# The first two query tiles made together, half of y at a time

## The chip, the cores and the metric

The kernel runs on one core of one Trainium2 chip. The metric is the device time of one execution in microseconds (us), lower is better. One execution was taken by the hardware profiler; its page, its trace and its own time are what the text below reads.

## The reference, cut to what matters

32 sequences of 32 tokens with 512 features go through one block of attention and a small feed-forward part, all in fp32. What the change touches is the step from x to the queries:

```
y   = x @ W.T + b + 2 * (x @ A[slot]) @ B[slot]     # base and adapter, slot per sequence
q   = rope(y @ Wq)      # 32 heads of 16
k,v = rope(y @ Wk), y @ Wv                          # 8 groups
ctx = softmax(mask(q k^T) / 4) v
x1  = x + ctx @ Wo
out = x1 + gated low-rank experts of x1             # top 2 of 4, through a second adapted product
```

## The kernel before

The work is cut into 4 groups (g) of 8 sequences, 256 tokens each. Features lie on the 128 partitions, so y of a group is 4 blocks (c) of 128 features by 256 tokens, and so is q: 4 tiles. To keep fp32 accuracy with the fast matmul type, each operand of a large product is held as a high part and a low part (what the high part leaves), and each product is three matmuls: high x high, high x low, low x high.

One y block therefore goes this way. TensorE sums it in PSUM (`y_base`, L1014, then `y_adapter`, L1022); blocks 0 and 1 are the halves of bank FR[0], blocks 2 and 3 those of FR[1]. ScalarE writes the high part with the bias (`y_high`, L338, matmul type, semaphore yT_h), VectorE the low part (`y_low`, L648, semaphore yT_l, one increment per block). `q_tile` (L1038) then multiplies with Wq over all four blocks: tiles 0 and 1 go to the halves of FR[0], which the y low parts of blocks 0 and 1 have just freed, tiles 2 and 3 to FR[1]. It waits until the low parts of all four blocks are there. The second tile of each bank raises q_ps. ScalarE then swaps partitions into qx (`q_swap`, L351, four copies), VectorE multiplies with cosine and sine, GpSimd adds (`q_sum`), and `scores` begins when all of q is there. `kv_tile` (L1048) makes k and v from the same y.

Each engine works through a list of steps in a fixed order that is written out by hand, one list per engine, with the groups interleaved: while group g is in its attention part, y of group g+1 is summed. An engine that waits holds back all that is listed behind. Around the change TensorE's list is:

- group 0: `y_adapter(0, 0)`, `y_adapter(0, 1)`, `keep_clock(6, ZB)` (six matmuls on zeros, in the profile the tile `still`), then the four q tiles, the two kv tiles and `y_base(1, 0)`
- group 1: `y_adapter(1, 1)`, `scores(0, 1)`, `p_transposes(0, 0, ZB)`, then the four q tiles
- group 2: two kv tiles, `scores(1, 1)`, `mid_logits` and `p_transposes` of earlier groups, then the q tiles
- group 3: `kv_tile(3, 1)`, then the q tiles

Other steps that the text names: ScalarE's list in group 1 is y_high(1, 0), y_high(1, 1), exp(0, 1), x_high(2, 0), wo_high(3), pt_copy(0, 0), x_high(2, 1), q_swap(1, 0), exp(0, 2), q_swap(1, 1), exp(0, 3), pt_copy(0, 1), kv_copy(1), k_swap(1). VectorE's `mask` and `top` mask the scores and take their maximum, GpSimd's `shift` (L530) subtracts it, ScalarE's `exp` (L374) follows, VectorE's `sums` (L714), GpSimd's `norm` (L525), and `p_transposes` (L1102) on TensorE. `x_low` (L639) is VectorE's low part of the next group's x. `mid_logits` (L1162) needs rows that SyncE loads for each label (`load_labels`, L196).

Of the kernel before, what the change touches and what calls it, by code (L numbers as in the profile page):

```python
# [15 lines left out]
KT = D // P  # L16
G = 4
SEQ = B // G
TOK = SEQ * T
# [43 lines left out]
def program(nc, xt, xn, idt, wt, wq, wkv, wo, w2, mix_in, small_in, lA, lB, consts, out):  # L63
    ctx = ExitStack()
    with ctx:
        def sb(name, shape, dt=F32):
            return ctx.enter_context(nc.sbuf_tensor(name, shape, dt))

        def sem(name):
# [9 lines left out]
        Wq = [sb(f"Wq{i}", [P, KT, PH, P], F32R) for i in "hl"]  # L79
# [13 lines left out]
        yS = [sb(f"yT{i}", [P, KT, TOK], F32R) for i in "hl"]  # L93
# [44 lines left out]
        FR, SMALL, SC, YB, ZB, XB = bank[0:2], bank[2], bank[3:5], bank[5], bank[6], bank[7]  # L138
# [11 lines left out]
        WT_h, WT_l, Wq_h, Wq_l, Wkv_h, Wkv_l, Wo_h, Wo_l, BT_l, xT_h, xT_l, yT_h, yT_l, cT_l = map(  # L150
            sem, "WT_h WT_l Wq_h Wq_l Wkv_h Wkv_l Wo_h Wo_l BT_l xT_h xT_l yT_h yT_l cT_l".split())
        h_ps, h_sb, y_half, y_ps, q_ps, q_sb, kv_ps, kv_sb, kx_sb, k_sin, q_sin, k_cos, q_cos = map(
            sem, "h_ps h_sb y_half y_ps q_ps q_sb kv_ps kv_sb kx_sb k_sin q_sin k_cos q_cos".split())
# [809 lines left out]
        def _(pe):  # L963
# [3 lines left out]
            def mm3(dst, lhsT, rhs, start, stop):  # L967
                mm(dst, lhsT[0], rhs[0], start, False)
                mm(dst, lhsT[0], rhs[1], False, False)
                return mm(dst, lhsT[1], rhs[0], False, stop)  # L970

            def keep_clock(n, dst):
                pe.wait_ge(blank, 1)
                for _ in range(n):
                    mm(dst[:, 0:P], still[:], still[:], True, True)
# [62 lines left out]
            def q_tile(g, q):  # L1038
                if g == 0:
                    pe.wait_ge(Wq_l, KT)  # L1040
                pe.wait_ge(yT_l, KT * (g + 1))
                dst = FR[q // 2][:, (q % 2) * TOK:(q % 2 + 1) * TOK]
                for c in range(KT):
                    i = mm3(dst, [w[:, c, q] for w in Wq], [z[:, c] for z in yS], c == 0, c == KT - 1)
                if q % 2:
                    i.then_inc(q_ps, 1)

            def kv_tile(g, n):  # L1048
                if g == 0:
                    pe.wait_ge(Wkv_l, 2)  # L1050
                pe.wait_ge(yT_l, KT * (g + 1))
                for c in range(KT):
                    i = mm3(SMALL[:, TOK * n:TOK * (n + 1)], [w[:, c, n] for w in Wkv], [z[:, c] for z in yS], c == 0, c == KT - 1)
                if n:
                    i.then_inc(kv_ps, 1)
# [46 lines left out]
            def p_transposes(g, j, dst):  # L1102
                if g == 0 and j < 2:
                    pe.wait_ge(RL_sb, KT)
                if 0 < g < G - 1 and j >= 2:
                    pe.wait_ge(fin_sb, TT * g)
                pe.wait_ge(normed, PAIRS * g + j + 1)
                for s in range(4):
                    i = tr(dst[:, P * s:P * (s + 1)], flat(ex[:, j])[:, P * s:P * (s + 1)])
                i.then_inc(pt_ps, 1)  # L1110
# [105 lines left out]
            y_adapter(0, 0)  # L1216
            y_adapter(0, 1)
            keep_clock(6, ZB)
            q_tile(0, 0)
            q_tile(0, 1)  # L1220
            q_tile(0, 2)
            q_tile(0, 3)
            kv_tile(0, 0)
            kv_tile(0, 1)
            y_base(1, 0)
            fold_router(0)
# [15 lines left out]
            y_adapter(1, 1)  # L1242
            scores(0, 1)
            p_transposes(0, 0, ZB)
            q_tile(1, 0)
            q_tile(1, 1)
            q_tile(1, 2)
            q_tile(1, 3)
            kv_tile(1, 0)
            p_transposes(0, 1, YB)  # L1250
            kv_tile(1, 1)
# [21 lines left out]
            mid_logits(0, 1, XB)  # L1273
            p_transposes(1, 0, ZB)
            p_transposes(1, 1, YB)
            q_tile(2, 0)
            q_tile(2, 1)
            q_tile(2, 2)
            q_tile(2, 3)
            v_spread(2)  # L1280
# [23 lines left out]
            mid_logits(1, 1, XB)  # L1304
            p_transposes(2, 0, ZB)
            kv_tile(3, 1)
            q_tile(3, 0)
            q_tile(3, 1)
            q_tile(3, 2)
            p_transposes(2, 1, YB)  # L1310
            mid_transpose(1, 0, XB)
# [90 lines left out]
```

## Time and profile before

| | |
|---|---|
| median of 3 runs | 161.06 us (160.15 to 162.93) |
| profiled execution, its own time | 160.41 us |
| its span, first to last instruction | 158.4 us |
| busy: TensorE, VectorE, ScalarE, GpSimd | 146.2, 99.4, 76.3, 65.3 us |
| mean granted TensorE clock | 1.000 |

Times in rows are microseconds from the start of the span, unless a row says ns. PE is TensorE, PEld its weight loads, DVE VectorE, ACT ScalarE, POOL GpSimd, SP SyncE (SPq: its issuing of DMAs). L with a number is a line of the kernel; where a helper issues an instruction the line is the helper's (L965 for most matmuls, L310 for copies on ScalarE). A timeline row is start, duration, engine, line, operation, output<-inputs, shapes and count; consecutive instructions alike are merged, and a bracket at the end is the idle time before them and what ended it. x4 means four instructions in a row. A fp32 matmul that is not of the fast type counts as two.

### The profile page before, as it was taken

The numbers are of one execution on the slowest core, as the hardware profiler recorded it, in microseconds if no ns is written. First come the engines' busy times: TensorE is split into PE (matmuls) and PEld (weight loads), VectorE is DVE, ScalarE is ACT, GpSimd is POOL, SyncE is SP. The second block draws the span as 40 slices with busy tenths as digits, with TensorE's granted clock in tenths as the row PEclk, the third lists the DMA queues.
The fourth block names the chain that finished last, engine by engine and source line by source line (L and its number), as shares of the span: only waits on it lengthen the run. The fifth ranks groups of instructions, "written<-read, shape, count | busy, mean of one in ns | idle before, by whom it ended". The sixth has DMA issues, their size and how long they took to land.

```text
span 158.4 us, 5011 instructions
## 1 busy us (share of the span) xinstructions
PE 146.2 (92%) x1970; PEld 135.1 (85%) x1970; DVE 99.4 (63%) x227; ACT 76.3 (48%) x152; POOL 65.3 (41%) x70
## 2 busy tenths in 40 slices
PE   6986699999979999999999999999999899789991
PEld 6985699998969998999999898999997689568761
DVE  0584455428849873166689794867838588708692
ACT  4642479921155994205397904261696450621410
POOL 1700000196252459620965584362774567610000
PEclk9999999999999999999999999999999999999999
DMA  5999993112154112430210013320002532134015
GB/s 143 370 289 387 411 388 70 37 41 45 41 169 153 43 42 58 135 115 0 84 57 0 4 55 117 107 73 4 0 0 76 201 110 106 39 114 136 1 66 199
DMA packets 14536, 17.76 MB, mean 112 GB/s; under 512 B 5762, under 2 KB 10370, under 8 KB 14258
## 3 DMA queue, kind: packets, MB, share of 16 engines
q1 hardware_dynamic: 13282, 15.23, 28.6%
q10 hardware_dynamic: 1040, 2.03, 4.2%
q8 instruction: 15, 0.25, 0.7%
q0 software_dynamic: 192, 0.20, 0.4%
q14 instruction: 7, 0.06, 0.1%
HBM read 10.90 MB, written 2.10 MB: 82 GB/s over the span
## 4 chain that ended last, share of the span: by engine, by line
PE 73%; DVE 8%; SPq 4%; ACT 4%; issue 3%; DMA 3%; POOL 1%; POOLq 1%; DVEq 0%
PE bank L965 55%; PE bank L997 12%; PE bank L978 4%; PE bank L1030 3%; DMA B<-lb 3%; DVE yTl L651 2%; DVE x L799 2%; ACT qx L310 1%; SPq L174 1%; SPq L175 1%; DVE mgT L794 1%; ACT yTh L343 1%; POOL qr L558 1%; SPq L177 1%; ACT PT L310 1%
## 5 line engine op out<-in xcount | busy, mean ns | idle before, releaser
L532 POOL TENSOR_TENSOR sm<-sm,mx 128x512 f32<-128x512 f32 x16 | 17.2, 1073 | 27.7 <-DVE mx L712 27.6
L527 POOL TENSOR_TENSOR ex<-ex,ri 128x512 f32<-128x512 f32 x16 | 17.3, 1089 | 10.0 <-DVE ri L718 9.9
L310 ACT COPY qx<-bank 32x512 f32<-32x512 f32 x32 | 18.5, 578 | 4.8 <-PE bank L965 4.3
L965 PE MATMUL bank<-yTh,Wqh 128*128 128x256 f32 x64 | 18.2, 285 | 2.4 <-DVE yTl L651 2.4
L376 ACT ACTIVATE ex<-sm 128x512 f32<-128x512 f32 x16 | 10.1, 633 | 17.1 <-POOL sm L532 16.9
L965 PE MATMUL bank<-yTl,Wqh 128*128 128x256 f32 x64 | 17.9, 280 | 0.0
L965 PE MATMUL bank<-yTh,Wql 128*128 128x256 f32 x64 | 17.9, 279 | 0.0
L997 PE MATMUL bank<-xTh,WTh 128*128 128x256 f32 x64 | 16.4, 289 | 0.0
L997 PE MATMUL bank<-xTl,WTh 128*128 128x256 f32 x64 | 16.1, 282 | 0.0
L310 ACT COPY PT<-bank 128x512 f32<-128x512 f32 (+1 forms) x17 | 9.6, 576 | 13.5 <-PE bank L978 11.8
L997 PE MATMUL bank<-xTh,WTl 128*128 128x256 f32 x64 | 15.9, 279 | 0.0
L707 DVE TENSOR_TENSOR sm<-bank,mixed 128x512 f32<-128x512 f32 x16 | 10.7, 674 | 7.0 <-PE bank L965 5.7
L965 PEld LDWEIGHTS bank<-yTh,Wqh 128*128 128x128 f32 x64 | 12.0, 188 | 2.8 <-issue 1.4
L965 PE MATMUL bank<-cTh,Woh 128*128 128x256 f32 x48 | 13.8, 288 | 0.0
L965 PE MATMUL bank<-cTh,Wol 128*128 128x256 f32 x48 | 13.3, 277 | 0.0
L965 PE MATMUL bank<-cTl,Woh 128*128 128x256 f32 x48 | 13.3, 277 | 0.0
L558 POOL TENSOR_TENSOR qr<-qkc,qks 128x512 f32<-128x512 f32 x8 | 10.5, 1317 | 5.5 <-DVE qkc L725 3.1
L716 DVE TENSOR_REDUCE su<-ex 128x16 f32<-128x512 f32 x16 | 10.8, 677 | 2.2 <-ACT ex L376 2.0
L539 POOL TENSOR_TENSOR qkc<-kv,mixed 128x256 f32<-128x256 f32 x4 | 2.9, 730 | 22.3 <-ACT kv L310 22.3
L965 PEld LDWEIGHTS bank<-yTl,Wqh 128*128 128x128 f32 x64 | 12.0, 188 | 0.0
L965 PEld LDWEIGHTS bank<-yTh,Wql 128*128 128x128 f32 x64 | 12.0, 187 | 0.0
L343 ACT ACTIVATE yTh<-bank,mixed 128x256 fp32r<-128x256 f32 x16 | 6.4, 474 | 11.5 <-PE bank L1030 11.4
(116 smaller groups left out, 396.7 us busy)
## 6 DMA issues: line engine op xcount, KB each, us to landing
RS<-RL SPq DMA_DIRECT2D x32, 136.0 KB, 2.0
xF<-xt SPq DMA_DIRECT2D x8, 256.0 KB, 3.2
out<-x SPq DMA_DIRECT2D x7, 256.0 KB, 2.1
Wqn<-wq ACTq DMA_DIRECT2D x2, 512.0 KB, 5.0
Wqn<-wo SPq DMA_DIRECT2D x1, 1024.0 KB, 6.4
Wn<-w SPq DMA_DIRECT2D x1, 1024.0 KB, 9.0
x<-small SPq DMA_DIRECT2D x1, 904.0 KB, 5.9
A<-la SPq DMA_DIRECT2D x28, 32.0 KB, 1.8
```

Source lines behind the costliest of these rows:

```text
L310: return nc.scalar.copy(dst, src)
L343: nc.scalar.activation(yS[0][:, c, :], FR[h][:, (c % 2) * TOK:(c % 2 + 1) * TOK], ACT.Identity, bias=bias[:, c:c + 1]).then_inc(yT_h, 1)
L376: nc.scalar.activation(flat(ex[:, j]), flat(sm[:, j % 2]), ACT.Exp, scale=HD ** -0.5).then_inc(exped, 1)
L527: nc.gpsimd.tensor_tensor(ex[:, j], ex[:, j], ri[:, j, :, None].broadcast_to((P, 2 * NG, T)), ALU.mult).then_inc(normed, 1)
L532: nc.gpsimd.tensor_tensor(sm[:, j % 2], sm[:, j % 2], mx[:, j, :, None].broadcast_to((P, 2 * NG, T)), ALU.subtract).then_inc(shifted, 1)
L558: nc.gpsimd.tensor_tensor(qr[:, :, s, :].rearrange("p s h t -> p h s t"), qkc[:, s].rearrange("p h (s t) -> p h s t", t=T), qks[:, s].rear ...
L707: V.tensor_tensor(sm[:, j % 2], SC[j % 2][:].rearrange("p (a s) -> p a s", s=T), small(C_CAUSAL, T)[:, None].broadcast_to((P, 2 * NG, T)), ...
L716: V.tensor_reduce(su[:, j], ex[:, j], AX.X, ALU.add).then_inc(summed, 1)
L965: return nc.tensor.matmul(dst, lhsT, rhs, start=start, stop=stop)
L978: return nc.tensor.transpose(dst, src, ident[0:n, 0:n])
L997: nc.tensor.matmul(FR[c // 2][:, (c % 2) * TOK:(c % 2 + 1) * TOK], WT[u][:, k, P * c:P * (c + 1)], xT[r][:, k], start=first, stop=False, s ...
L1030: i = nc.tensor.matmul(FR[b][:, n * TOK + P * e:n * TOK + P * (e + 1)], B1[g % 2][rows, P * (2 * b + n):P * (2 * b + n + 1)], hT[rows, P * ...
```

## The change

In each group q tiles 0 and 1 are made by one function. It goes over the first two blocks of y for both tiles, then over the last two for both. Ahead of each half it waits for the low parts of that half's blocks only. The 24 matmuls are those of the two tiles before, in another order; `start` is set on the first one of the bank alone, and q_ps is raised once at the end, as before. The calls are replaced in all four groups; nothing else changes.

```diff
+            def q_pair(g):
+                if g == 0:
+                    pe.wait_ge(Wq_l, KT)
+                for half in range(2):
+                    pe.wait_ge(yT_l, KT * g + 2 * (half + 1))
+                    for q in range(2):
+                        for c in (2 * half, 2 * half + 1):
+                            for u, r in ((0, 0), (0, 1), (1, 0)):
+                                i = nc.tensor.matmul(FR[0][:, q * TOK:(q + 1) * TOK], Wq[u][:, c, q], yS[r][:, c],
+                                                     start=c == 0 and q == 0 and u == 0 and r == 0, stop=c == KT - 1 and u == 1,
+                                                     skip_group_check=True)
+                i.then_inc(q_ps, 1)
+
...
             keep_clock(6, ZB)
-            q_tile(0, 0)
-            q_tile(0, 1)
+            q_pair(0)
             q_tile(0, 2)
             q_tile(0, 3)
...
             p_transposes(0, 0, ZB)
-            q_tile(1, 0)
-            q_tile(1, 1)
+            q_pair(1)
             q_tile(1, 2)
...
-            q_tile(2, 0)
-            q_tile(2, 1)
+            q_pair(2)
...
-            q_tile(3, 0)
-            q_tile(3, 1)
+            q_pair(3)
```

## Rows read from the trace of the kernel before

**Rows 1.** The page: busy time by engine, and TensorE's granted clock in 40 slices.
```profile
PE 146.2 (92%) x1970; PEld 135.1 (85%) x1970; DVE 99.4 (63%) x227; ACT 76.3 (48%) x152; POOL 65.3 (41%) x70
...
PEclk9999999999999999999999999999999999999999
```

**Rows 2.** The page: chain that ended last, by line.
```profile
PE bank L965 55%; PE bank L997 12%; PE bank L978 4%; PE bank L1030 3%; DMA B<-lb 3%; DVE yTl L651 2%; DVE x L799 2%; ACT qx L310 1%; SPq L174 1%; SPq L175 1%; DVE mgT L794 1%; ACT yTh L343 1%; POOL qr L558 1%; SPq L177 1%; ACT PT L310 1%
```

**Rows 3.** Waits of TensorE: engine, tile and line, releaser, total us, times, longest.
```profile
PE bank L965 <- DVE yTl L651: 2.4, 2, 1.2
```

**Rows 4.** Timeline of TensorE, groups 0 and 1: start, us, what.
```profile
16.43 1.60 PE L965 MATMUL bank<-still 128*128 128x128 f32 x12
19.27 0.36 PE L965 MATMUL bank<-yTh,Wqh 128*128 128x256 f32 x1 [1.24 <-DVE yTl L651]
...
46.09 0.66 PE L978 MATMUL bank<-K,ex 128*128 128x128 f32 x4
47.88 0.38 PE L965 MATMUL bank<-yTh,Wqh 128*128 128x256 f32 x1 [1.13 <-DVE yTl L651]
```

**Rows 5.** Timelines of VectorE and TensorE, group 2.
```profile
73.59 0.88 DVE L651 SCALAR_TENSOR_TENSOR yTl<-bank,mixed,yTh 128x256 fp32r<-128x256 f32 x2 [0.37 <-ACT yTh L343]
...
81.50 0.36 PE L965 MATMUL bank<-yTh,Wqh 128*128 128x256 f32 x1
```

**Rows 6.** Timeline of VectorE, y low parts of groups 0 and 1.
```profile
17.46 0.88 DVE L651 SCALAR_TENSOR_TENSOR yTl<-bank,mixed,yTh 128x256 fp32r<-128x256 f32 x2 [1.76 <-ACT yTh L343]
...
18.65 0.47 DVE L651 SCALAR_TENSOR_TENSOR yTl<-bank,mixed,yTh 128x256 fp32r<-128x256 f32 x1
...
46.16 0.87 DVE L651 SCALAR_TENSOR_TENSOR yTl<-bank,mixed,yTh 128x256 fp32r<-128x256 f32 x2 [1.96 <-ACT yTh L343]
...
47.35 0.47 DVE L651 SCALAR_TENSOR_TENSOR yTl<-bank,mixed,yTh 128x256 fp32r<-128x256 f32 x1
```

**Rows 7.** Timeline of TensorE, products of a q tile.
```profile
19.46 0.28 PE L965 MATMUL bank<-yTl,Wqh 128*128 128x256 f32 x1
...
20.76 0.28 PE L965 MATMUL bank<-yTh,Wqh 128*128 128x256 f32 x1
```

**Rows 8.** Timeline of ScalarE, group 0.
```profile
22.37 2.34 ACT L310 COPY qx<-bank 32x512 f32<-32x512 f32 x4 [1.12 <-PE bank L965]
```

**Rows 9.** Timeline of ScalarE, group 1.
```profile
51.01 2.35 ACT L310 COPY qx<-bank 32x512 f32<-32x512 f32 x4 [1.59 <-PE bank L965]
53.38 0.63 ACT L376 ACTIVATE ex<-sm 128x512 f32<-128x512 f32 x1
54.03 2.35 ACT L310 COPY qx<-bank 32x512 f32<-32x512 f32 x4
```

**Rows 10.** Timelines of GpSimd and VectorE, group 1; durations of L641 (ns, min/median/max).
```profile
48.78 1.05 POOL L527 TENSOR_TENSOR ex<-ex,ri 128x512 f32<-128x512 f32 x1 [2.45 <-DVE ri L718]
52.26 1.05 POOL L532 TENSOR_TENSOR sm<-sm,mx 128x512 f32<-128x512 f32 x1 [2.43 <-DVE mx L712]
...
49.17 1.22 DVE L641 TENSOR_TENSOR xTl<-xF,xTh 128x512 fp32r<-128x512 f32 x1
...
L641 DVE TENSOR_TENSOR xTl<-xF,xTh x8: 679/684/1220, 6.4 to 88.8; 128x512 fp32r<-128x512 f32 x8
```

**Rows 11.** The normalization of the fourth pair, and its transposes.
```profile
59.49 1.05 POOL L527 TENSOR_TENSOR ex<-ex,ri 128x512 f32<-128x512 f32 x1
...
61.21 0.60 PE L978 MATMUL bank<-K,ex 128*128 128x128 f32 x4
```

**Rows 12.** Later steps of group 1 on TensorE and GpSimd.
```profile
65.16 1.04 POOL L564 TENSOR_TENSOR Kbd<-kr,mixed 128x512 f32<-128x512 f32 x1
...
67.57 1.05 PE L965 MATMUL bank<-Kbd,qr 64*128 64x128 f32 x14
```

**Rows 13.** Timelines of TensorE and SyncE, the tail.
```profile
134.65 1.16 PE L965 MATMUL bank<-RS,x 128*32 128x68 f32 x64
...
123.93 13.09 SPq L204 DMA_DIRECT2D RS<-RL  x9
```


## The prediction

> **What bounds the kernel now.** I read the page first. TensorE is busy 92% of the span, the next engine 63%, and the granted clock is at full speed (2.4 GHz) in every slice up to the end [rows 1]. The chain that ended last says the same by time: the four matmul lines carry 55 + 12 + 4 + 3 = 74% of the span, the y low part on VectorE 2% and the y high part on ScalarE 1% [rows 2]. So this kernel is one long matmul queue, and a change in it is worth the idle time that it closes in that queue, if nothing behind has a fixed time. Then the list of waits: TensorE's longest item is its wait for the y low parts (L651), 2.4 us in only two waits, the longest 1.2 [rows 3]. The timeline places them. In group 0 the dummy matmuls end at 16.43 + 1.60 = 18.03, and the first q matmul starts at 19.27 after 1.24 idle. In group 1 the transposes end at 46.09 + 0.66 = 46.75 and q starts at 47.88 after 1.13 idle [rows 4]. Groups 2 and 3 are not among the two waits: in group 2 the last y low part ends at 73.59 + 0.88 = 74.47 and the first q matmul starts at 81.50 with no idle [rows 5], and in group 3 it is the same pattern.
>
> **What the change does, part by part.** It adds and removes no matmul: per group, two tiles of 4 blocks x 3 products are 24 matmuls before and after, all with 256 columns and the same operands, in another order. One semaphore wait per group is added, q_ps still comes with the last of the 24, and q tiles 2 and 3, which write the other bank, stay behind.
>
> *Group 0.* The first two y low parts end at 17.46 + 0.88 = 18.34, the last at 18.65 + 0.47 = 19.12 [rows 6]. Before, the first q matmul started 19.27 - 19.12 = 0.15 after the last part. Now it needs only the second: 18.34 + 0.15 = 18.49, and TensorE is free from 18.03. Gain 19.27 - 18.49 = 0.78.
> Is there enough work in front of the second wait? Consecutive products start (20.76 - 19.46) / 11 = 0.118 us apart [rows 7]. Twelve take 1.41 us, so the second half is due at about 18.49 + 0.08 + 1.41 = 19.98 (the first of a run takes 0.08 more, 19.27 to 19.46), 0.86 after the last y part. So the added second wait is satisfied when TensorE reaches it, and the whole 0.78 stays. What is queued behind that wait is all of TensorE's work and, through q_ps, ScalarE's swap; if the cover of 0.86 were gone, every us of lateness would be a us of span.
>
> *Group 1.* The first two parts end at 46.16 + 0.87 = 47.03, the last at 47.35 + 0.47 = 47.82 [rows 6]; gain 0.79, TensorE is free at 46.75, and the second half again has its 1.41 us of cover. Together 1.57 us after q_pair(1).
>
> *Groups 2 and 3.* Both waits are long satisfied (in group 2 by 81.50 - 74.47 = 7.0 us [rows 5]); the order alone changes. Price 0.
>
> *The added waits and the other order themselves.* A wait that is satisfied: the first q matmul of group 2 stands behind one and has no idle in front of it [rows 5]. From above, the first matmul of a run costs 0.08 more than its successors [rows 7], so four waits are 0 to 0.32 us; I take 0, since group 2's is the nearest row. Writing FR[0] while ScalarE and VectorE read FR[1] is new in groups 0 and 1. Group 2's y low parts run while TensorE is busy with projections, at 0.88 for two, as in groups 0 and 1 where it is idle (0.88, 0.87) [rows 5, 6]: 0. Alternating between the two halves of a bank is what the y products already do, with the same steps; no row suggests a cost. A gain from it is excluded by the count and the common shape of the products.
>
> **Does the shift survive what has a fixed time?** Everything behind in the queue has to move with it. In group 0, ScalarE's q swap starts 0.78 earlier, at 21.59 instead of 22.37, and its queue is free from 22.37 - 1.12 = 21.25 [rows 8]. From there the engines wait for TensorE or for each other, so all of group 0 moves by 0.78.
> In group 1 one thing does not. ScalarE's first swap moves from 51.01 to 49.44 and ends at 51.79. Behind it in ScalarE's queue stands exp(0,2), which needs GpSimd's subtraction, 52.26 + 1.05 = 53.31 before [rows 9, 10]. That comes from group 0's masks behind y low on VectorE, whose time is not changed by group 1's gain: it moves by 0.78 only, to 52.53. So exp starts at about 52.6 instead of 53.38, and the second swap at 53.25 instead of 54.03: ScalarE idles some 0.75 us, and its chain (second swap, exp, kv copy, k swap) is 0.78 early, not 1.57. Who waits for that? The second swap releases VectorE's sine product, the sums behind it, and GpSimd's normalization, which ends at 59.49 + 1.05 = 60.54, now 59.76; the transposes of the fourth pair start at 61.21 and would now start at 59.64 [rows 11]. They slip by 59.76 + 0.05 - 59.64, about 0.15. GpSimd's further list for group 1 (k, q sums, blocks) ends at 65.16 + 1.04 = 66.20, now 65.42, for scores at 67.57, now 66.15 [rows 12]. One more thing there has a time of its own, the load of x(2), which ScalarE takes in front of its first swap; it had 1.59 us idle between the two [rows 9], so even if the load does not come a bit earlier, the 0.78 that ScalarE loses on it fits. So the sum is 0.78 + 0.79 - 0.15 = 1.42; bounds 0.78 (the second gain lost) and 1.57.
>
> **The tail.** SyncE's row of label loads for group 2 runs 123.93 + 13.09 = 137.02, and mid_logits of group 2 starts at 134.65 close to its end [rows 13]; but its start hangs on the stored tiles of group 1, which TensorE releases, so it moves too. TensorE's own waits in the tail are on engines that TensorE released.
>
> **Against which time.** The profiled execution took 160.41 (span 158.40, 2.01 around it); its forecast is 160.41 - 1.42 = 158.99. The median of the three runs is 161.06, 0.65 above, and they spread from 160.15 to 162.93. I put the reported time half way between: 158.99 + 0.33 = 159.3. A change of 2% (3.2 us) is about what a measurement of this kernel can tell from none.
>
> **Rivals.**
> *Only group 0's gain arrives.* For it: ScalarE and GpSimd are 0.78 early, not 1.57, from 52 to 66, and VectorE's queue there is dense. Against: where that work crosses back to TensorE it had 61.21 - 60.54 = 0.67 and 67.57 - 66.20 = 1.37 to spare [rows 11, 12]. Gain 0.78, time 160.41 - 0.78 + 0.33 = 159.96.
> *The two waits close, but nothing arrives.* A later wait grows by what was won: label loads that did not start earlier (until 137.02) would hold mid_logits(2) [rows 13], and in the tail each engine waits for another with nothing to spare. Against: all of them descend from TensorE. The variant that the first half's wait is no earlier, for a reason of ordering, is excluded by the two y low ends [rows 6]. Time 160.41 + 0.33 = 160.74.
> *Slower: VectorE and GpSimd fall onto each other.* In group 1 the two change their phase by up to 0.79. A collision has a price in the trace: x_low at 49.17 took 1.22 beside a GpSimd operation that began at 48.78, where the median of the eight is 0.68 [rows 10]: 0.54. The place is the list of ten GpSimd operations from 52 to 66, which would have 66.15 - 65.42 = 0.73 to spare before scores. The second new collision there begins to eat the gain, and the fourth (4 x 0.54 = 2.16, over 0.73 + 1.42 = 2.15) ends later than before; six give 160.41 + (3.24 - 2.15) + 0.33 = 161.8. Against: both engines work through fixed lists, and most neighbours keep their distance. The Trainium skill, SBUF — State Buffer, section "SBUF: two separate sides", has this as an exclusive lock between VectorE with two SBUF inputs and GpSimd, held for the whole instruction. The trace agrees: x_low ended at 49.17 + 1.22 = 50.39, 0.56 after the GpSimd operation's end at 49.83, not far from its own length of 0.68, so it stood nearly still until then; as an estimate by that page, a new overlap costs up to the whole 1.05 of a GpSimd operation rather than 0.54, and three would do.
>
> **Chances.** Forecast 0.62, only group 0's gain 0.15, nothing arrives 0.14, slower 0.05, something better than 1.57 (a later wait vanishes) 0.04. The range takes in the first three with the spread of the runs: low 159.3 less about 0.9 (the runs lie up to 0.9 under the median) = 158.4, high 160.74 + 0.65 (what lies between the profiled execution and the median) = 161.4. Only a gain over 3.2 is faster by 2%: 0.03. Slower by 2% needs 164.3: 0.02. Within 2%: 0.95.
>
> **What the new profile would show.** First q matmul at about 18.5 and 47.1 - 0.8 = 46.3 on the old clock; the wait for L651 down from 2.4 to about 0.85 us (0.46 and 0.33 left), no idle between the halves; group 0's ScalarE swap near 21.6; ScalarE idle for some 0.75 before exp(0,2); fourth transposes near 59.8; q of groups 2 and 3 without idle; a span near 157.0. I am wrong if the halves are split by a gap, if q matmuls step wider than 0.118, or if waits from 119 on grow by what the first two lost.

## The result, and the profile after

Over 22 executions the changed kernel has a median of 160.09 us, beside 161.00 for 22 of the kernel before. The ratio is 0.9924, 95% interval 0.99 to 0.9948: 1.22 us of 161 (0.84 to 1.61). That is faster, and by less than 2%. Medians here are over all executions, and by them the gain is 0.91; ratios leave out the executions that lie over 1.5% above the fastest of their kernel, so the two need not agree. One execution of the changed kernel took 281.14 us, the other 21 took 158.29 to 161.50; it was not profiled, it came once, and its cause is open.

The profiled execution of the changed kernel took 161.27, its span 159.2. That is longer than before, so it can't be read by its end. It has to be read step by step. The page first:

```profile
PE 147.7 (93%) x1970; PEld 136.1 (85%) x1970; DVE 99.2 (62%) x227; ACT 76.2 (48%) x152; POOL 65.3 (41%) x70
...
PEclk9998699999999999999999999999999999999999
...
PE bank L965 47%; PE bank L997 12%; PE bank L1056 7%; PE bank L1030 4%; PE bank L978 4%; DMA B<-lb 3%; DVE x L799 2%; ACT qx L310 1%; SPq L174 1%; DVE yTl L651 1%; SPq L175 1%; DVE mgT L794 1%; ACT yTh L343 1%; POOL qr L558 1%; SPq L177 1%
```

The same 1970 matmuls, the same share of matmul lines in the chain (47 + 12 + 7 + 4 + 4 = 74%, the pair now having its own line L1056), and L651 down from 2% to 1% [rows 2]. New is the clock: it is 0.6 in the fifth slice, where before had full speed everywhere [rows 1]. The waits of TensorE, in us, times, longest:

```profile
PE bank L965 <- DMA B<-lb: 2.5, 1, 2.5
...
PE bank L1056 <- DVE yTl L651: 0.8, 2, 0.5
```

The wait for the y low parts went from 2.4 to 0.8, still two waits [rows 3]. The timeline of TensorE from the first slot's rows to the first q tiles, and then in group 1 (start, duration, what, idle before):

```profile
13.97 0.72 PE L965 MATMUL bank<-xF,A 128*32 128x64 f32 x32 [2.51 <-DMA B<-lb]
...
16.23 2.47 PE L1030 MATMUL bank<-hT,B 64*128 64x128 f32 x16
18.64 1.60 PE L965 MATMUL bank<-still 128*128 128x128 f32 x12
20.70 0.36 PE L1056 MATMUL bank<-yTh,Wqh 128*128 128x256 f32 x1 [0.46 <-DVE yTl L651]
20.90 0.28 PE L1056 MATMUL bank<-yTl,Wqh 128*128 128x256 f32 x1
...
22.19 0.28 PE L1056 MATMUL bank<-yTh,Wqh 128*128 128x256 f32 x1
...
23.49 0.28 PE L1056 MATMUL bank<-yTh,Wql 128*128 128x256 f32 x1
...
47.52 0.66 PE L978 MATMUL bank<-K,ex 128*128 128x128 f32 x4
48.52 0.38 PE L1056 MATMUL bank<-yTh,Wqh 128*128 128x256 f32 x1 [0.35 <-DVE yTl L651]
```

What to see: the dummies end at 18.64 + 1.60 = 20.24 and q starts 0.46 later, where it was 1.24; in group 1 it is 0.35, where it was 1.13 [rows 4]. The thirteenth product, the first behind the second wait, starts at 22.19 in step with its neighbours. VectorE's rows show why:

```profile
19.68 1.66 DVE L651 SCALAR_TENSOR_TENSOR yTl<-bank,mixed,yTh 128x256 fp32r<-128x256 f32 x4 [3.22 <-ACT yTh L343]
...
47.59 1.66 DVE L651 SCALAR_TENSOR_TENSOR yTl<-bank,mixed,yTh 128x256 fp32r<-128x256 f32 x4 [1.96 <-ACT yTh L343]
```

The last low part ends at 21.34, 0.85 before that product. And the start: the slot's rows came late (13.97 for 13.21 before), and behind the 2.51 us of idle the 16 adapter products took 2.47 us instead of 1.50. By stretches (columns: length, busy us of TensorE, its weight loads, VectorE, ScalarE and GpSimd, then granted clock, DMA share and GB/s):

```profile
15.00:17.00 2.00, 2.00 (x14) 1.78 (x14) 1.46 (x3) 0.00 (x0) 0.00 (x0) 0.53 1.00 414
17.00:18.50 1.50, 1.43 (x14) 1.09 (x10) 0.00 (x0) 0.00 (x0) 0.00 (x0) 0.50 1.05 369
```

From about 15.1 to 18.5 the clock was granted at its lower level (1.2 GHz). So this execution had lost 2.21 us before the change's first instruction: 0.76 by the late rows and 1.45 by the clock.

To keep this out of the comparison, I subtract: the start of each TensorE step less the start of the same step in before, in the profiled executions. A kernel that only starts late has a constant in its row; each real gain or loss is a step. "Dummies" is keep_clock(6), ahead of the change. p_transposes(0, 2) and (0, 3) are the transposes of the third and the fourth pair, "behind them" is v_spread(1), the step that follows: what the fourth pair loses is the difference of these two columns.

| | dummies | q group 0 | scores(0,0) | q group 1 | p_transposes(0,2) | behind them | scores(1,0) | last step |
|---|---|---|---|---|---|---|---|---|
| after | 2.21 | 1.43 | 1.43 | 0.64 | 0.64 | 0.72 | 0.71 | 0.86 |
| e4, after again | 2.50 | 1.72 | 1.72 | 0.93 | 0.94 | 1.02 | 1.01 | 0.99 |
| e1, order only | 2.85 | 2.85 | 2.85 | 2.85 | 2.85 | 2.86 | 2.86 | 2.82 |
| e2, group 0 only | 2.59 | 1.81 | 1.44 | 1.43 | 1.44 | 1.45 | 1.44 | 1.43 |
| e3, group 1 only | 1.48 | 1.47 | 1.11 | 0.32 | 0.32 | 0.42 | 0.31 | 0.33 |
| e5, tile by tile | 1.97 | 1.19 | 1.21 | 0.43 | 0.50 | 0.52 | 0.41 | 0.28 |
| e6, swap first | 0.70 | -0.08 | -0.08 | -0.87 | -1.28 | -1.28 | -1.28 | -1.32 |
| e7, fold in the wait | -0.18 | -0.87 | -1.23 | -2.03 | -2.03 | -1.78 | -1.79 | -1.61 |
| e8, kept warm | 0.01 | -0.78 | -0.77 | -1.55 | -1.52 | -0.85 | -0.86 | -0.90 |
| e9, warm, x(2) early | 0.54 | -0.25 | -0.25 | -1.04 | -1.03 | -0.94 | -0.95 | -0.97 |
| e10, before, warm | 0.29 | 0.29 | 0.29 | 0.28 | 0.29 | 0.30 | 0.29 | 0.48 |
| e11, all together | 0.04 | 0.53 | 1.17 | 0.39 | 0.39 | 0.39 | 0.39 | 0.57 |
| e12, x(2) early | 0.54 | -0.26 | -0.62 | -1.41 | -1.40 | -1.31 | -1.32 | -1.35 |

For after: 2.21 to 1.43 is 0.78 in group 0, 1.43 to 0.64 is 0.79 in group 1, then 0.08 is lost at the fourth transposes and 0.03 of that comes back; 0.69 stand before project(2, 0), a net gain of 2.21 - 0.69 = 1.52. The last 0.17 is lost in the late projections and is no part of the change (last section).

The loss at the fourth transposes is small, and it has to be read from the right row. First before, the eight transposes of the third and the fourth pair, then the last four of them alone; then after, the eight:

```profile
60.83 1.09 PE L978 MATMUL bank<-K,ex 128*128 128x128 f32 x8
...
61.32 0.60 PE L978 MATMUL bank<-K,ex 128*128 128x128 f32 x4
```
```profile
61.47 1.17 PE L978 MATMUL bank<-K,ex 128*128 128x128 f32 x8
```

The fourth pair begins at 61.32 in before. The row at 61.21 that the prediction worked with [rows 11] begins in the middle of the eight: it holds the last transpose of the third pair and three of the fourth. In after the eight take 1.17 instead of 1.09, and that is the whole slip: the start of the fourth pair, 61.98, is 0.66 behind before's, where the third pair had 0.64, and the first transpose behind the wait takes 0.06 more than without one.

### The profile page after: what moved, and what is told of

It is laid out like the page before. It is cut to its first block, busy times and chain, and to the rows that moved or that the text cites. A ratio compares the mean times of both kernels' runs of the same rounds, so it can differ in the third digit from the quotient of the medians.

```text
span 159.2 us, 5010 instructions
## 1 busy us (share of the span) xinstructions
PE 147.7 (93%) x1970; PEld 136.1 (85%) x1970; DVE 99.2 (62%) x227; ACT 76.2 (48%) x152; POOL 65.3 (41%) x70
## 3 DMA queue, kind: packets, MB, share of 16 engines
q10 hardware_dynamic: 1040, 2.03, 4.0%
## 4 chain that ended last, share of the span: by engine, by line
PE 74%; DVE 7%; SPq 4%; ACT 4%; DMA 3%; issue 3%; POOL 1%; POOLq 1%; DVEq 0%
PE bank L965 47%; PE bank L997 12%; PE bank L1056 7%; PE bank L1030 4%; PE bank L978 4%; DMA B<-lb 3%; DVE x L799 2%; ACT qx L310 1%; SPq L174 1%; DVE yTl L651 1%; SPq L175 1%; DVE mgT L794 1%; ACT yTh L343 1%; POOL qr L558 1%; SPq L177 1%
## 5 line engine op out<-in xcount | busy, mean ns | idle before, releaser
L310 ACT COPY qx<-bank 32x512 f32<-32x512 f32 x32 | 18.5, 578 | 4.8 <-PE bank L1056 3.6
L997 PEld LDWEIGHTS bank<-xTh,WTh 128*128 128x128 f32 x64 | 11.1, 188 | 1.0 <-issue 0.8
L997 PEld LDWEIGHTS bank<-xTh,WTl 128*128 128x128 f32 x64 | 11.5, 196 | 0.0
L689 DVE TENSOR_TENSOR cTl<-bank,cTh 128x512 fp32r<-128x512 f32 x8 | 5.4, 679 | 9.3 <-ACT cTh L310 9.3
L997 PEld LDWEIGHTS bank<-xTl,WTh 128*128 128x128 f32 x64 | 11.1, 188 | 0.1
L651 DVE SCALAR_TENSOR_TENSOR yTl<-bank,mixed,yTh 128x256 fp32r<-128x256 f32 x16 | 6.7, 477 | 7.1 <-ACT yTh L343 7.1
L712 DVE TENSOR_REDUCE mx<-sm 128x16 f32<-128x512 f32 x16 | 10.8, 674 | 0.1
```

The costliest lines, as they stand in the source:

```text
L310: return nc.scalar.copy(dst, src)
L651: V.scalar_tensor_tensor(out=yS[1][:, c], in0=FR[h][:, (c % 2) * TOK:(c % 2 + 1) * TOK], scalar=bias[:, c:c + 1], in1=yS[0][:, c].bitcast( ...
L712: V.tensor_reduce(mx[:, j], sm[:, j % 2], AX.X, ALU.max).then_inc(maxed, 1)
L997: nc.tensor.matmul(FR[c // 2][:, (c % 2) * TOK:(c % 2 + 1) * TOK], WT[u][:, k, P * c:P * (c + 1)], xT[r][:, k], start=first, stop=False, s ...
```

## The experiments

### e1: the order alone

```diff
-                    pe.wait_ge(yT_l, KT * g + 2 * (half + 1))
+                    pe.wait_ge(yT_l, KT * (g + 1))
```

> The new order of the 24 matmuls in all four groups, but both waits of q_pair ask for all four y low parts, so nothing may start early. My theory (the gain is the earlier start, the order is free): the first q matmul stands behind the fourth low part with 1.24 us idle in group 0 and 1.13 us in group 1 as before, q matmuls step 0.118 us, ratio to before 1.000 (between 0.998 and 1.002). Rival that the order or the added waits have a price: up to 4 x 0.08 = 0.3 us slower, ratio 1.002. Rival that the order itself is what gains: ratio 0.992 as for the whole change.

Measured: 161.16 beside 161.04, ratio 0.998 (0.9936 to 1.0024). TensorE's waits are those of before, and so is the idle in front of the first product:

```profile
PE bank L1056 <- DVE yTl L651: 2.4, 2, 1.2
```
```profile
22.12 0.36 PE L1056 MATMUL bank<-yTh,Wqh 128*128 128x256 f32 x1 [1.25 <-DVE yTl L651]
```

Its shift is 2.85 from the dummies to scores(1, 0) and 2.82 at the end. So the other order, the added waits, and writing one bank in halves cost nothing within 0.01 us per group, in all four groups; all of the gain comes from what is waited for.

### e2 and e3: one group alone

```diff
-            q_pair(1)
+            q_tile(1, 0)
+            q_tile(1, 1)
```

e2 keeps the pair in group 0 only, e3 in group 1 only; the other three groups have their two calls of q_tile again.

> The pair in group 0 alone, the old q tiles in groups 1 to 3. My theory: 0.46 us idle before the first q matmul of group 0 instead of 1.24, all behind it moved by 0.78 us, ScalarE's whole group 1 too, 1.13 us idle left in group 1; time 0.78 under before, ratio 0.995. Rival (only group 0's gain ever arrives): the same 0.995 here, and the whole change no better than this kernel. Rival (nothing arrives): ratio 1.000, a wait behind 119 us grown by 0.78.

> The pair in group 1 alone, the old q tiles in the other groups. My theory: idle before group 1's first q matmul 0.34 us instead of 1.13, TensorE then 0.79 us early, but exp(0,2) keeps its time in front of ScalarE's second swap, so the transposes of the fourth pair slip by about 0.17 us and 0.62 us arrive; ratio 0.996. Rival (the chain over ScalarE and GpSimd eats group 1's gain): ratio 1.000. If VectorE and GpSimd fell onto each other, ratio above 1.000.

Measured: e2 160.26, ratio 0.9927 (0.9884 to 0.997); e3 160.86, ratio 0.9968 (0.9925 to 1.0012). The intervals hardly part the two, and e2's ratio is no worse than that of the whole change (0.9924): by the times alone, "only group 0's gain arrives" is not excluded. The rows decide it. In e2:

```profile
21.08 0.36 PE L1056 MATMUL bank<-yTh,Wqh 128*128 128x256 f32 x1 [0.46 <-DVE yTl L651]
...
49.31 0.39 PE L965 MATMUL bank<-yTh,Wqh 128*128 128x256 f32 x1 [1.14 <-DVE yTl L651]
```

and in e3:

```profile
20.74 0.36 PE L965 MATMUL bank<-yTh,Wqh 128*128 128x256 f32 x1 [1.24 <-DVE yTl L651]
...
48.20 0.38 PE L1056 MATMUL bank<-yTh,Wqh 128*128 128x256 f32 x1 [0.35 <-DVE yTl L651]
```

Each wait shrinks only where the pair is. e2 gains 2.59 - 1.81 = 0.78 and loses nothing behind: its fourth transposes keep their distance. e3 gains 1.11 - 0.32 = 0.79 and slips 0.10 at the fourth transposes (0.32 to 0.42). So the slip that I had subtracted is real and belongs to group 1's pair. That e3 stands at 0.31 again at scores(1, 0) is no recovery: the y_base products of group 2 in between ran with the shorter matmul spacing, as did the stretches in front of scores(0, 0) that give the drops of 0.37 and 0.36 (last section).

### e4: the changed kernel once more

No edit: it gives a second profile of the changed kernel, next to e1 to e3.

> The changed kernel again, for a profile in which TensorE's clock is not lowered between 15 and 19 us, and as the measure for the other three. My theory: 1.42 us under before, ratio 0.991, which is the sum of group 0 alone (0.78) and group 1 alone (0.62) to within 0.05 us; no lower clock in the profile, span near 157.0 us. Rival (only group 0's gain): as e2_group0_only, ratio 0.995.

Measured: 160.08, ratio 0.9929 (0.9887 to 0.9972). The start again waited 2.39 us for the slot's rows and again ran on at half clock (the adapter products took 2.16). So this profile has the lower clock too, against what I expected. Gains 0.78 and 0.79, slip 0.08, net 2.50 - 0.99 = 1.51. The two profiles agree to 0.01 where it matters.

### e5: without the pair

Tile 0 alone waits in two steps; tiles 1 to 3 wait for all of y as before.

```diff
             def q_tile(g, q):
...
-                pe.wait_ge(yT_l, KT * (g + 1))
+                if q:
+                    pe.wait_ge(yT_l, KT * (g + 1))
...
                 for c in range(KT):
+                    if q == 0 and c % 2 == 0:
+                        pe.wait_ge(yT_l, KT * g + c + 2)
```

> No pair: the old q tiles one after the other, but tile 0 of each group waits for two low parts in front of its first two blocks and for the others in front of its last two; tiles 1 to 3 as before. The first half then holds 6 matmuls instead of 12, 0.71 us of work. My theory (all that counts is the earlier start, and 0.71 us of work just bridges the 0.78 us to the last low part): idle before the first q matmul 0.46 and 0.34 us as with the pair, a gap of 0 to 0.1 us between the halves of tile 0, so 0 to 0.2 us slower than the pair, ratio to before 0.991 to 0.993. Rival (the 12 matmuls of the pair are needed, because a wait in the middle drains the engine): a gap of 0.2 us and more in each group, ratio 0.994 and up.

Measured: 160.23, ratio 0.9943 (0.9897 to 0.999), the rival's figure, but the interval takes in both. Here only six products stand between the two waits. In group 1 TensorE's rows, around the seventh product, are

```profile
48.31 0.39 PE L965 MATMUL bank<-yTh,Wqh 128*128 128x256 f32 x1 [0.35 <-DVE yTl L651]
...
49.00 0.28 PE L965 MATMUL bank<-yTh,Wql 128*128 128x256 f32 x1
49.12 0.36 PE L965 MATMUL bank<-yTh,Wqh 128*128 128x256 f32 x1
49.31 0.28 PE L965 MATMUL bank<-yTl,Wqh 128*128 128x256 f32 x1
```

and the last low part ends at 47.38 + 1.66 = 49.04. The seventh product comes in step, and its neighbour 0.19 behind it instead of 0.12: a gap of at most 0.08, and 0.02 in group 0. Net 1.97 - 0.41 = 1.56 at scores(1, 0), of which 0.11 is the shorter matmul spacing in the same y_base products as in e3. So six products (0.7 us) all but bridge what is missing, and the pair's twelve are more cover than is needed. The mechanism is the split wait; the pairing is insurance against a later low part.

### e6: the second swap ahead of exp(0, 2)

```diff
             q_swap(1, 0)
-            exp(0, 2)
             q_swap(1, 1)
+            exp(0, 2)
```

> The changed kernel with ScalarE's exp(0,2) behind its second swap of group 1 instead of in front of it. My theory (exp(0,2) kept its time and held the swap): ScalarE no longer idles about 0.7 us between the two swaps, the second swap starts right behind the first's end, kv copy and k swap come about 0.8 us earlier against TensorE, the transposes of the fourth pair no longer wait for GpSimd. The whole gives back at most the slip of 0.15 us, of which the profile of the change showed 0.13 at the transposes and 0.05 behind scores(1,0): so ratio 0.991 to 0.992, no difference that timing can tell from the change. Rival (the chain is held by VectorE or GpSimd, not by exp): the transposes of the fourth pair stay where they are.

Measured: 159.84, ratio 0.992 (0.9863 to 0.9977). ScalarE in e6:

```profile
50.04 2.35 ACT L310 COPY qx<-bank 32x512 f32<-32x512 f32 x4 [0.71 <-PE bank L1056]
52.76 2.35 ACT L310 COPY qx<-bank 32x512 f32<-32x512 f32 x4 [0.37 <-PE bank L965]
55.13 1.15 ACT L376 ACTIVATE ex<-sm 128x512 f32<-128x512 f32 x2
```

In after, the same place reads

```profile
51.65 2.35 ACT L310 COPY qx<-bank 32x512 f32<-32x512 f32 x4 [0.81 <-PE bank L1056]
54.77 0.63 ACT L376 ACTIVATE ex<-sm 128x512 f32<-128x512 f32 x1 [0.77 <-POOL sm L532]
55.42 2.35 ACT L310 COPY qx<-bank 32x512 f32<-32x512 f32 x4
```

The 0.77 of idle that the prediction put there (0.75) is gone in e6, the normalization is in time, and the fourth transposes no longer slip (-1.28 and -1.28 around them; the eight take 1.09 again). That shows the cause of the slip. A slip of 0.08 is 0.0005 of the time, too little for the runs to show. (The step from -0.87 to -1.28 ahead of them is matmul spacing again.)

### e7: useful work in place of half the dummies

The matmuls that fold the label's second factor (x8 in the profile) stood later in group 0, behind fold_router(0). Here they stand in front of the first q and three of the six dummy matmuls are left out.

```diff
-            keep_clock(6, ZB)
+            keep_clock(3, ZB)
+            fold_label_b()
             q_pair(0)
...
-            fold_label_b()
...
             def fold_label_b():
+                pe.wait_ge(d_small, 16)
```

> The changed kernel, and in group 0 three of the six dummies in front of q_pair(0) are replaced by the eight matmuls of fold_label_b, which stood behind y_base(1,0) and need only a load that has landed by then. My theory (TensorE's queue is the bound, so 0.89 us of real work that moves into a wait comes off the end): first q matmul of group 0 where it is in the change, y_base(1,0) too, everything behind fold_router 0.89 us earlier; ratio to before 0.9924 - 0.0055 = 0.987. Rival (a step with a time of its own behind it, the load of w2, the label sums on VectorE or the load of x(2), takes it back): part of the 0.89 us turns up as idle of TensorE before fold_router, scores(0,0) or in group 2, ratio 0.990 to 0.992. If the load of the small weights is late in a run, q_pair(0) is held.

Measured: 159.07, the lowest median of all; ratio 0.9915 (0.987 to 0.9961), in the rival's range and not at my 0.987. TensorE:

```profile
16.24 0.94 PE L965 MATMUL bank<-still 128*128 128x128 f32 x6
17.49 1.11 PE L965 MATMUL bank<-x 128*128 128x68 f32 x8 [0.31 <-DMA x<-small]
18.40 0.36 PE L1056 MATMUL bank<-yTh,Wqh 128*128 128x256 f32 x1
...
36.34 1.16 PE L965 MATMUL bank<-Kbd,qr 64*128 64x128 f32 x16 [0.45 <-POOL qr L558]
```

The fold fills the rest of the wait, and its 0.89 us are gone from their old place. But scores(0, 0) now waits for GpSimd's rotated q: of 0.89 only 0.89 - 0.52 = 0.37 stays (-0.87 to -1.23). Group 1 gains its 0.79 as always; at the fourth transposes 0.25 is lost for 0.08 in after, and in e7 ScalarE had waited 1.03 and 0.37 for the halves of x(2). With TensorE 0.87 us earlier the next engine's list becomes the bound here, first in group 0.

### e8, e9 and e12: an early start, and the load of x(2)

e8 adds seven dummy matmuls (x14 in the profile) in front of adapter_in(0), where TensorE otherwise idles for the slot's rows. e9 is e8 with SyncE's load of x(2) ahead of the slot rows of group 2. e12 has the early load alone.

```diff
             y_first_low(2)
+            keep_clock(7, ZB)
             adapter_in(0)
...
             next_slots(1)
-            next_slots(2)
             load_x(2)
+            next_slots(2)
```

> The changed kernel with seven more dummies (14 matmul instructions, 1.87 us) in front of adapter_in(0), in the wait for the first adapter slots. In three of the profiles of this case TensorE idled 2.5 to 3.0 us there and its granted clock then was at half for 3.41 us, from about 15 to 19 us; in the profile of before it idled 1.82 us and the clock stayed up. My theory for the spread of the runs (the lowered clock follows the idle of this wait, and costs up to 1.4 us): no half clock before the end of the span, span near 157.0 us even with a late slot, median 0.5 to 1 us under the change, ratio to before 0.986 to 0.989. Rival (the clock falls for another reason, or its fall costs nothing because the wait behind it absorbs it): a half clock again, ratio 0.992.

> The kernel e8_keep_warm with one more edit: SyncE issues the load of x(2) ahead of the 16 adapter loads of group 2 instead of behind them, some 14 us earlier. In e8's profile ScalarE waited for that load 0.47 us before its first half and 1.39 us before its second, its first swap of group 1 began at 50.75 instead of 49.4, and the transposes of the fourth pair idled 0.68 us. My theory now (the load of x(2) has a fixed time, which I had set aside as hidden, and it takes back part of group 1's gain whenever the start of the kernel is early): no wait of ScalarE for that load, first swap at about 49.4, idle before those transposes 0.1 us, end of the last step 0.5 to 0.65 us earlier than in e8. The fastest runs fall from 159.2 to about 158.6, ratio to before 0.988 to 0.991. Rival (exp(0,2) on ScalarE is the cause of the whole slip): transposes still idle 0.5 us and more.

> The changed kernel with the early load of x(2) alone, no dummies. My theory: where the start is early the gain of e9 over e8 is here as well, where slots land late (x(2) was no bound in the profile of the change) nothing changes; so the fastest runs gain about 0.5 us and the median 0.1 to 0.4 us against e4_after_again, ratio to before 0.989 to 0.992. Rival (earlier traffic of x(2) delays the adapter loads or the load of w2): ratio 0.993 or more.

Measured: e8 159.77, ratio 0.9961 (0.9915 to 1.0006); e9 159.77, ratio 0.9914 (0.9877 to 0.9951); e12 159.56, ratio 0.9883 (0.9827 to 0.994). e8 misses its forecast of 0.986 to 0.989, and the fastest of e9 (159.41) misses the 158.6 expected. In 7 of the 30 executions of e8, e9 and e11 some of the time lies outside the span: it is 2.35 to 3.79 longer than the span, against about 2.0 (at most 2.21) in all the others, and e9's profiled execution is one of the seven (160.57, span 157.4). Why is open; it makes these three kernels look worse than their spans do. e8's profile is the cleanest look at the change, since its start is that of before (shift 0.01):

```profile
11.22 1.72 PE L965 MATMUL bank<-still 128*128 128x128 f32 x14
13.22 0.72 PE L965 MATMUL bank<-xF,A 128*32 128x64 f32 x32 [0.28 <-DMA B<-lb]
...
15.01 1.50 PE L1030 MATMUL bank<-hT,B 64*128 64x128 f32 x16
...
18.49 0.36 PE L1056 MATMUL bank<-yTh,Wqh 128*128 128x256 f32 x1 [0.45 <-DVE yTl L651]
...
46.33 0.38 PE L1056 MATMUL bank<-yTh,Wqh 128*128 128x256 f32 x1 [0.35 <-DVE yTl L651]
```

18.49 and 46.33 are the forecast's 18.49 and 46.3. But only 0.90 of 1.57 arrives at the end. ScalarE in e8:

```profile
47.08 0.62 ACT L310 CAST xTh<-xF 128x512 fp32r<-128x512 f32 x1 [0.48 <-DMA xF<-xt]
...
50.10 0.62 ACT L310 CAST xTh<-xF 128x512 fp32r<-128x512 f32 x1 [1.39 <-DMA xF<-xt]
50.75 2.35 ACT L310 COPY qx<-bank 32x512 f32<-32x512 f32 x4
53.20 0.63 ACT L376 ACTIVATE ex<-sm 128x512 f32<-128x512 f32 x1
```

The second half of x(2) landed at about 50.1, so ScalarE's first swap, which q released at about 49.4, stands behind a cast that waits for a DMA, starts at 50.75 and delays exp(0, 2), the second swap and the normalization. TensorE pays at the fourth transposes:

```profile
60.42 0.66 PE L978 MATMUL bank<-K,ex 128*128 128x128 f32 x4 [0.45 <-POOL ex L527]
```

There the shift jumps from -1.52 to -0.85, a loss of 0.67 for 0.08 in after. e9 and e12 remove the wait. In e12:

```profile
48.14 0.65 ACT L310 CAST xTh<-xF 128x512 fp32r<-128x512 f32 x1
49.60 2.35 ACT L310 COPY qx<-bank 32x512 f32<-32x512 f32 x4 [0.82 <-PE bank L1056]
52.73 0.63 ACT L376 ACTIVATE ex<-sm 128x512 f32<-128x512 f32 x1 [0.77 <-POOL sm L532]
```

The cast has no wait, the swap is released by TensorE again, and the slip is back to 0.09. Net: e9 0.54 + 0.97 = 1.51; e12 0.54 + 1.35 = 1.89, less 0.36 from shorter matmul spacing in front of scores(0, 0), 1.53. Both of them have the slot's rows 0.5 us later than before, but so has e5 without the early load, which is issued only at about 32; so that is no price of it. The medians of e8 and e9 are equal, on two chips: what the early load is worth over many executions is not shown.

### e10: the kernel before with the same dummies

```diff
             y_first_low(2)
+            keep_clock(7, ZB)
             adapter_in(0)
```

> The kernel before with the seven dummies in front of adapter_in(0), and nothing of the change. My theory (the runs of the kernel before at 162 us and over are those whose clock was lowered between 15 and 19 us): no run with a mean clock under 0.99, few runs at 162 or more, median 160.5 us; 1.24 and 1.13 us idle before the first q matmuls as in before. Rival (the dummies themselves cost time, since they hold a slot that has landed): all runs later by 0.2 to 0.5 us. Against e8_keep_warm it gives the worth of the change without lowered clocks: 0.9 us by e8's profile, 1.42 by my sum.

Measured: 160.78 beside 160.88, ratio 1.0005 (0.9966 to 1.0044), idle 1.24 and 1.14 in front of q as before. So e8's gain is not the dummies'. Against e10 the changed kernel with the same dummies (e9, on the same chip, with x(2) early besides) is 1.01 faster by the medians. What the dummies seem to do is steady the start: the mean granted clock fell below 0.991 in none of 24 executions of e8 and e9 and in 1 of 12 of e10, but in 7 of 22 of after and 5 of 12 of e4. (In e12, without them, it did in none of 6, in e11, with them, in 1 of 6.) My theory that the executions at 162 and over are those with the lowered clock fails here: three of e10's twelve took 162.29, 163.19 and 162.39, the first two at a mean clock of 0.995. Something else makes them slow, and it is open.

### e11: all of it

After with e6's, e7's and e9's edits, and on ScalarE kv_copy(0) and k_swap(0) ahead of b_high and wo_high(1), against e7's wait at scores(0, 0).

```diff
-            b_high()
             kv_copy(0)
-            wo_high(1)
             k_swap(0)
+            b_high()
+            wo_high(1)
             wo_high(2)
```

> The changed kernel with all that helped, and one thing more: fold_label_b in the wait of group 0, the load of x(2) early, exp(0,2) behind the second swap, the dummies in the slot wait, and ScalarE's kv_copy(0) and k_swap(0) ahead of b_high and wo_high(1), because in e7's profile scores(0,0) idled 0.61 us for GpSimd's q sum, whose list begins with the kv copy. My theory: first q matmul at 18.4 as in e8, fold worth 0.89 us and all of it kept, group 1's gain whole; against before 1.57 + 0.89 = 2.4 us in the profile, median near 158.2 us, ratio 0.983 to 0.986. Rival (GpSimd's list of group 0 is the bound however its start moves): scores(0,0) still idles 0.5 us, ratio 0.987 to 0.990.

Measured: 159.25 over 6 executions (158.28 to 160.96), ratio 0.9847 (0.9791 to 0.9904), the best ratio. The profiled one is the slowest of the six. In it the small weights, which the fold needs, were late, and a half clock stretch followed:

```profile
18.88 1.11 PE L965 MATMUL bank<-x 128*128 128x68 f32 x8 [1.48 <-DMA x<-small]
...
20.20 0.41 PE L1056 MATMUL bank<-yTh,Wql 128*128 128x256 f32 x1
20.41 0.41 PE L1056 MATMUL bank<-yTh,Wqh 128*128 128x256 f32 x1
```

Behind it the edits work: scores(0, 0) has none of e7's 0.45 idle, the step from there to q of group 1 is 1.17 to 0.39 = 0.78, and no slip follows. The price of the fold in the wait is that it hangs on a DMA that is not always there. The ratios of e11 and e12 are better than the change's, but each rests on six executions, e12's interval holds the change's 0.9924, and e11's upper end (0.9904) touches its interval. e11's ratio is the one forecast (0.983 to 0.986), its median 1 us above the forecast 158.2.

## Why the prediction was right

**The time.** Forecast 159.3 (158.4 to 161.4), measured 160.09; forecast gain 1.42, measured 1.22 (0.84 to 1.61) by the ratio, 0.91 by the medians, and 1.51 and 1.52 by step in the two profiles of the changed kernel. I had set the reported time between the profiled execution and the median of three, which is 0.26 too low as a base (160.74); over 22 executions the kernel before stands at 161.0. The other half us between forecast and median is gain that the rows show and the medians do not.

**The two waits.** Two waits of 1.24 and 1.13 became 0.46 and 0.35, gains of 0.78 and 0.79 against 0.78 and 0.79 forecast. e2 and e3 show each alone.

**The cover.** 0.86 forecast, 0.85 measured, no gap between the halves in any of the profiles. e5 shows that half the work in front of the second wait would have done, at a price of 0.02 and 0.08.

**Waits, order, groups 2 and 3.** Price 0 taken, up to 0.32 as the bound; e1 shows 0, at a shift that stays within 0.03 over the whole span.

**The slip of 0.15.** Its place and its cause were right (gone in e6), and so was that it stays. Its size was not: it is 0.08 in after and e4, 0.09 in e9 and e12, 0.10 in e3, and 0.01 to 0.03 of it comes back. I had compared GpSimd's end with 61.21, which is the last transpose of the third pair. With 61.32 my own sum gives 59.76 + 0.05 - 59.75 = 0.06, the gain 1.51, and the time to spare that I held against the first rival is 61.32 - 60.54 = 0.78 and not 0.67. So 1.57 - 0.08 + 0.03 = 1.52 is what after shows, and the forecast of 1.42 is 0.1 low by this row.

**The load of x(2).** This is the other term that I mis-sized. I wrote that it is hidden even if it does not come a bit earlier, since ScalarE had 1.59 us idle between it and the swap. The idle stood behind the cast, but the load's landing is not fixed at its place in the profile of before: in e8, with SyncE issuing it 0.2 us earlier than in before, the second half came at about 50.1, in before at 48.0. 0.61 of the 1.57 is lost by it (0.90 in e8 for 1.51 in e9). From issue to landing the second half took 5.5 us in e8, 4.2 in e7, 4.6 and 4.7 in e2 and e3, and 3.2 to 3.6 in before, after and e4. So it is not the early start alone: e2 and e3 started late and had ScalarE wait for it too (0.37 and 0.65, 0.83 and 0.43), but those waits fit into ScalarE's later idle and cost TensorE 0.02 at most. In after and e4 ScalarE did not wait for it, and in e9 and e12 it is issued earlier. This explains the lower end of the measured gain in part; how many executions lose by it is open, since only one of each kernel was profiled.

**The rivals.** "Nothing arrives" and "slower" are out: labels and tail moved along (e4: 1.01 at scores(1, 0), 0.99 at the end), and no new collision of VectorE and GpSimd appears as a step in the table; in after the two are as busy as in before (99.2 for 99.4, 65.3 for 65.3). "Only group 0's gain" describes the size in e8 (0.90), but not for its reason: GpSimd's density did not hold TensorE, a DMA in front of ScalarE's queue did.

**The range.** It held, and its upper part was needed for the base and the load rather than for the rivals. But it was 3.0 us wide and holds the kernel before (161.00) as well, so that it held says little; what carries the prediction is the rows.

## What to carry to other kernels

Where one engine bounds everything, look at each wait for how much of what it waits for the next instruction needs; a wait on a part is free if the work behind it bridges the rest, and here six products would nearly have bridged it. After moving the bound queue earlier, look for what stands in other queues with a time of its own, transfers first: an idle gap behind a load in one profile does not say how late that load can come. A gain of 1% is read from the starts of the same steps in both traces, not from the ends of two executions that begin differently. And when a narrow window is laid over a longer series of like instructions, its row can begin in another step than the one meant: look at the whole series once.

## What the runs showed of the hardware

**The clock after an idle start.** In after, TensorE idled 2.51 us and then ran for 3.4 us at the half clock, which cost 1.45 us; e4 the same behind 2.39 (its shift went from 1.07 to 2.50, 1.43), e5 behind 2.22, e1 behind 2.73 and e2 behind 2.84. In before 1.82 us of idle left the clock at full [rows 1], in e3 2.28 did, and in e6 2.55 (its 16 adapter products took 1.50, as in before). So the idle time alone does not tell. With dummies in it the clock stayed at full in the profiles of e8, e9 and e10; in e11 it fell behind another idle, of 1.48. In e11's half clock stretch the 256-column products stand 0.21 apart instead of 0.118.

**Two spacings at full clock.** The same 256-column products stand apart by two amounts, in e2 and in after here:

```profile
21.27 0.28 PE L1056 MATMUL bank<-yTl,Wqh 128*128 128x256 f32 x1
...
23.76 0.28 PE L1056 MATMUL bank<-yTh,Wql 128*128 128x256 f32 x1
```

(23.76 - 21.27) / 22 = 0.1132 in e2, where after has (23.49 - 20.90) / 22 = 0.1177 in the same 24 products. The Trainium skill, TensorE: Matmul & The Clock Gate, section "Wait — 56ns, not 53.3ns?", gives columns / 2.4 GHz plus about 2.5 ns, which as an estimate by that page would be 0.109 for 256; neither value is that. The shorter one appears in stretches of some executions (some 20 to 29 us in e2, e3 and e12, group 2's y_base in e3 and e5, from group 1's q on in e6; the late projections in before but not in after, 0.17 us), for both kernels. Its cause is open; it moves the end by up to 0.4 us and has nothing to do with the change.
